# One attention kernel: tables of the group loop redrawn, and the rows of the maxima split on GpSimd and copied on ScalarE

## The reference, cut to what matters

```
scores = einsum('bhqd,bhkd->bhqk', q, k) / sqrt(16)
scores = where(causal, scores, -inf)
attn = softmax(scores, axis=-1)
y = einsum('bhqk,bhkd->bhqd', attn, v)
```

## Time and profile before

| | us |
|---|---|
| median of 3 runs (lowest, highest) | 811.58 (811.36, 812.0) |
| the profiled execution | 810.96 |
| its span | 809.2 |
| granted TensorE clock, mean of the span | 0.998 of full speed |

### The profile page before, as it was taken

One profiled execution on the slowest core, in us unless ns is written; L12 is line 12 of the kernel. 1 busy time (PEld: TensorE's weight loads), 2 busy tenths in 40 slices (PEclk: granted clock), 3 DMA queues, 4 the chain that ended last, 5 costly groups with the idle time before them and its releaser, 6 DMA issues.

```text
span 809.2 us, 15844 instructions
## 1 busy us (share of the span) xinstructions
PE 793.1 (98%) x5286; PEld 534.4 (66%) x5286; DVE 690.7 (85%) x2103; ACT 439.1 (54%) x843; POOL 303.1 (37%) x387
## 2 busy tenths in 40 slices
PE   9999999999999999999999999999999999999996
PEld 6788876876545555555555455555448888888886
DVE  4874767678899999999999999999698888888877
ACT  5333322323479988888988888999861111111110
POOL 0213121221224453535436454555442724334231
PEclk9999999999999999999999999999999999999999
DMA  8316183364613544343454344351321101011111
GB/s 292 118 36 199 41 240 99 98 190 117 149 42 71 107 98 88 85 104 80 90 119 111 77 107 111 74 132 44 105 97 48 46 33 52 26 52 37 42 40 40
DMA packets 44242, 75.53 MB, mean 93 GB/s; under 512 B 13388, under 2 KB 15116, under 8 KB 44172
## 3 DMA queue, kind: packets, MB, share of 16 engines
q1 hardware_dynamic: 44028, 74.51, 35.0%
q10 hardware_dynamic: 144, 0.13, 0.0%
HBM read 48.30 MB, written 21.23 MB: 86 GB/s over the span
## 4 chain that ended last, share of the span: by engine, by line
PE 84%; DVE 6%; ACT 3%; issue 2%; DMA 1%; SPq 1%; POOL 0%; DVEq 0%
PE bank L1879 17%; PE bank L1763 12%; PE bank L1748 11%; PE bank L554 11%; PE bank L556 11%; PE bank L555 11%; ACT pt L1114 2%; PE bank L1692 2%; PE bank L2026 2%; PE bank L1758 2%; PE bank L1708 1%; PE bank L1774 1%; PE bank L1759 1%; DMA ks<-k_parts 1%; PE bank L1947 1%
## 5 line engine op out<-in xcount | busy, mean ns | idle before, releaser
L1114 ACT ACTIVATE pt<-bank 128x512 f32<-128x512 f32 x576 | 305.2, 623 | 52.7 <-PE bank L1748 49.5
L1257 DVE CUSTOM_DVE_ANT_0 bank<-bank,cmask 128x256 f32<-128x256 f32 (+3 forms) x456 | 202.7, 491 | 21.6 <-PE bank L1763 20.2
L1748 PE MATMUL bank<-qs,ks 50*128 50x512 f32 (+3 forms) x768 | 206.1, 376 | 0.9
L1763 PE MATMUL bank<-ks,qs 48*128 48x512 f32 (+3 forms) x712 | 190.3, 392 | 1.9 <-DMA ks<-k_parts 0.9
L1763 PEld LDWEIGHTS bank<-ks,qs 48*128 48x128 f32 x712 | 101.1, 184 | 90.5 <-DVE mx L1260 28.1
L1879 PE MATMUL bank<-pt,vb 128*32 128x512 f32 (+3 forms) x1536 | 157.0, 496 | 0.2 <-ACT pt L1114 0.2
L881 POOL TENSOR_SCALAR_AFFINE_SELECT pt<-pt 128x512 f32<-128x512 f32 (+1 forms) x160 | 85.1, 551 | 158.4 <-ACT pt L1114 158.4
L1748 PEld LDWEIGHTS bank<-qs,ks 50*128 50x128 f32 x768 | 114.9, 185 | 36.1 <-ACT pt L1114 24.9
L1260 DVE TENSOR_REDUCE mx<-bank 128x1 f32<-128x512 f32 x200 | 130.6, 679 | 1.5 <-PE bank L1763 1.1
L800 POOL TENSOR_TENSOR part<-rope,part 128x1024 fp32r<-128x1024 f32 x16 | 38.2, 2388 | 163.8 <-ACT part L972 163.8
L926 POOL TENSOR_TENSOR g<-comb,hr 128x1024 f32<-128x1024 f32 x16 | 30.8, 1925 | 107.4 <-DVE comb L1508 101.9
(11 more groups left out here) (196 smaller groups left out, 1542.6 us busy)
## 6 DMA issues: line engine op xcount, KB each, us to landing
qs<-q_parts SPq DMA_DIRECT2D x34, 256.0 KB, 3.9
ks<-k_parts SPq DMA_DIRECT2D x34, 256.0 KB, 4.3
q_parts<-part SPq DMA_DIRECT2D x32, 256.0 KB, 3.4
k_parts<-part SPq DMA_DIRECT2D x32, 256.0 KB, 3.3
qs<-q_parts SPq DMA_DIRECT2D x34, 128.0 KB, 4.8
ks<-k_parts SPq DMA_DIRECT2D x34, 128.0 KB, 3.4
yv<-yts SPq DMA_DIRECT2D x128, 32.0 KB, 2.3
rspread<-dens SPq DMA_DIRECT2D x64, 64.0 KB, 2.3
```

The source lines that it names most:

```text
L1114: act.activation(pt[k % PT_BUFS][:, h], score_out(g, c), ACT.Exp, scale=float(HD) ** -0.5).then_inc(S("exp_done"), 1)
L1257: last = ve.tensor_tensor_reduce(blk, blk, cmask[:, BANK - nk * P:], 1.0, NEG, ALU.add, ALU.max, mx[m][:, 0, h, qt:qt + 1])
L1748: last = pe.matmul(score_out(g, c)[:, col:col + n_], ks[slot_of(g)][r0:r0 + KX, h // 2, kb * P:(kb + 1) * P], qs[slot_of(g)][r0:r0 + KX, h ...
L1763: last = pe.matmul(out[:, col:col + nk * P], qs[slot][r0:r0 + KR, pr, qt * P:(qt + 1) * P], ks[slot][r0:r0 + KR, pr, k0 * P:(k0 + nk) * P] ...
```

## The change: what it does

1. `BANK_ORDER`, `MAX_AT` and `VALUES_AT` are redrawn. The value steps stood at 8, 12, 17, 22, 25, 27, 32, 35, 38, 41 and stand at 8, 11, 17, 20, 23, 26, 29, 32, 38, 41; the steps (1, [5, 7]) and (1, [1]) change places. The number of tiles, scores and value steps is as it was. `CALC_AT` and `ROWS_AT` are still slots 28 and 30; the last tile of the next group is now issued in chunk 25 (it was 26), the transposition in chunk 30 as before, but now at its start and straight behind the value step of chunk 29.
2. For groups 1 to 15 VectorE only joins the maxima (`join_maxima`). GpSimd makes the high part as a plain rounded copy and the low part by a subtraction, not negated (`split_maxima`, ahead of the work of chunk 26).
3. ScalarE copies the transposed rows from the bank to `mrow` with the factor -1 (`copy_rows`, ahead of the exponential of chunk 30). VectorE's copy is gone. Group 0 is done as before (`first_rows`).
4. The waits follow: TensorE's transposition waits for `rows_low`, SyncE's DMAs and the next user of the bank wait for `rows_copied`, and `reads_before` leaves these uses out.

```diff
-BANK_ORDER = [[[2, 1, 0, 3, EXCESS, 5, JOINED, 4, 6], [2, 0, 6, 1, 5, 4, EXCESS, 3, JOINED]],
-              [[2, 4, EXCESS, 3, 6, 0, 5, JOINED, 1], [3, 4, 6, 0, 5, EXCESS, 2, 1, JOINED]]]
+BANK_ORDER = [[[0, 3, 2, 1, EXCESS, 4, 5, JOINED, 6], [6, 2, 3, 5, 4, 0, EXCESS, 1, JOINED]],
+              [[EXCESS, 5, 6, 0, JOINED, 3, 2, 4, 1], [2, 6, 5, EXCESS, 1, 3, JOINED, 4, 0]]]
...
+JOIN_AT = 26
...
-VALUE_STEPS = [(0, [0]), (0, [2]), (0, [1, 3]), (1, [0]), (1, [6]), (1, [5, 7]), (1, [1]), (1, [4]), (1, [2]), (1, [3])]
+VALUE_STEPS = [(0, [0]), (0, [2]), (0, [1, 3]), (1, [0]), (1, [6]), (1, [1]), (1, [5, 7]), (1, [4]), (1, [2]), (1, [3])]
...
-VALUES_AT = [8, 12, 17, 22, 25, 27, 32, 35, 38, 41]
+VALUES_AT = [8, 11, 17, 20, 23, 26, 29, 32, 38, 41]
...
-MAX_AT = [0, 0, 2, 3, 4, 5, 5, 6, 8, 8, 8, 9, 10, 11, 12, 13, 15, 16, 17, 17, 19, 20, 20, 22, 22, 23, 25, 26, 29, 30, 30, 32, 33, 34, 35, 35]
+MAX_AT = [0, 0, 2, 3, 3, 4, 5, 6, 6, 7, 8, 9, 11, 11, 12, 13, 14, 15, 16, 17, 19, 19, 19, 21, 22, 23, 24, 25, 26, 28, 30, 31, 32, 33, 35, 35]
...
+            def split_maxima(g):
+
+                gp.wait_ge(S("max_joined"), g + 1)
+                rows = mall[:].rearrange("p (a n) -> p a n", a=2)
+                gp.tensor_copy(mneg[:, :, 0], rows).then_inc(S("rows_high"), 1)
+                gp.wait_ge(S("rows_high"), g)
+                gp.tensor_tensor(mneg[:, :, 1], rows, mneg[:, :, 0], ALU.subtract).then_inc(S("rows_low"), 1)
...
+                    if g + 1 < G and c == JOIN_AT:
+                        split_maxima(g + 1)
...
+            def copy_rows(g, use):
+
+                act.wait_ge(S("max_full"), use + 1)
+                act.activation(mrow[g % 3][:], max_out(use)[0:2 * HG * QT, 0:P], ACT.Copy, scale=-1.0
+                               ).then_inc(S("rows_copied"), 1)
...
+                    if g + 1 < G and c == rows_chunk(g):
+                        copy_rows(g + 1, use_of(g, ROWS_AT))
...
-                ve.wait_ge(S("max_joined"), g + 1)
-                rows = mall[:].rearrange("p (a n) -> p a n", a=2)
-                ve.tensor_scalar(mneg[:, :, 0], rows, -1.0, None, ALU.mult).then_inc(S("max_neg_high"), 1)
-                ve.wait_ge(S("max_neg_high"), g + 1)
-                ve.scalar_tensor_tensor(out=mneg[:, :, 1], in0=rows, scalar=-1.0, in1=mneg[:, :, 0],
-                                        op0=ALU.mult, op1=ALU.subtract).then_inc(S("max_negated"), 1)
```

More of the change, by code:

```diff
@@ L249 @@
 EXCESS_USES = [use_of(_g, n) for _g in range(G) for n in slots_with(excess, _g)]
+ROWS_USES = [use_of(_g, ROWS_AT) for _g in range(G - 1)]
 EXCESS_CHUNK = {n: EXCESS_LAG + max(c for c in range(SCORE_BANKS) if FIRST[c] <= n) for n in slots_with(excess, EXCESS_FROM)}
@@ L254, in reads_before, with rows_chunk @@
 def reads_before(use):
-    return use - sum(u < use for u in EXCESS_USES)
+    return use - sum(u < use for u in EXCESS_USES + ROWS_USES)
+def rows_chunk(g):
+    slots = FIRST if g else [first_slots(c) for c in range(SCORE_BANKS)]
+    return max(c for c in range(SCORE_BANKS) if slots[c] <= ROWS_AT)
 def excess_before(g):
@@ L652, in store_max @@
             def store_max(g, use):
-                sp.wait_ge(S("max_read"), reads_before(use) + 1)
+                if g == 0:
+                    sp.wait_ge(S("max_read"), use + 1)
+                else:
+                    sp.wait_ge(S("rows_copied"), g)
                 for par in range(2):
@@ L1262, in max_bank, with join_maxima @@
                 last.then_inc(S("max_read"), 1)
-            def max_rows(g, use):
+            def join_maxima(g, use):
                 if EXCESS_FROM <= g and SLOT_CLEARED[0] + 3 <= g:
@@ L1270, in max_rows, with first_rows @@
                                  ).then_inc(S("max_joined"), 1)
-                ve.wait_ge(S("max_joined"), g + 1)
+            def first_rows(use):
+                join_maxima(0, use)
+                ve.wait_ge(S("max_joined"), 1)
                 rows = mall[:].rearrange("p (a n) -> p a n", a=2)
                 ve.tensor_scalar(mneg[:, :, 0], rows, -1.0, None, ALU.mult).then_inc(S("max_neg_high"), 1)
-                ve.wait_ge(S("max_neg_high"), g + 1)
+                ve.wait_ge(S("max_neg_high"), 1)
                 ve.scalar_tensor_tensor(out=mneg[:, :, 1], in0=rows, scalar=-1.0, in1=mneg[:, :, 0],
                                         op0=ALU.mult, op1=ALU.subtract).then_inc(S("max_negated"), 1)
-            def copy_rows(g, use):
                 ve.wait_ge(S("max_full"), use + 1)
-                ve.tensor_copy(mrow[g % 3][:], max_out(use)[0:2 * HG * QT, 0:P]
-                               ).then_inc(S("max_read"), 1)
+                ve.tensor_copy(mrow[0][:], max_out(use)[0:2 * HG * QT, 0:P]).then_inc(S("max_read"), 1)
             ve.wait_ge(S("c_ld"), 16 * 4)
@@ L1315, in _ @@
                 max_bank(0, w, w)
-            max_rows(0, NMX)
-            copy_rows(0, NMX)
+            first_rows(NMX)
             ve.wait_ge(S("roped"), HEAD["roped"] + 4 * TILES)
@@ L1330, in ve_group @@
                     if slot == CALC_AT and g + 1 < G:
-                        max_rows(g + 1, use_of(g, slot))
+                        join_maxima(g + 1, use_of(g, slot))
                     if slot == FIRST[INVERT_AT] and g > 0:
@@ L1336, in ve_group @@
                         ve.memset(mx[g % 3][:, 0, :, QT - 1], NEG).then_inc(S("slot_cleared"), 1)
-                    if not held(g, slot) or slot in slots_with(excess, g):
+                    if slot == ROWS_AT or not held(g, slot) or slot in slots_with(excess, g):
                         continue
[L1339 to L1343, removed]
+                    n, w = max_tile(slot)
+                    max_bank(g + n, w, use_of(g, slot))
             for w in range(LEAD):
@@ L1725, in free_bank @@
                     pe.wait_ge(S("excess_copied"), EXCESS_USES.index(use - MAX_BUFS) + 1)
+                elif use - MAX_BUFS in ROWS_USES:
+                    pe.wait_ge(S("rows_copied"), ROWS_USES.index(use - MAX_BUFS) + 1)
                 else:
@@ L1779, in trans_rows @@
                     keep_on(out)
-                pe.wait_ge(S("max_negated"), g + 1)
+                if g == 0:
+                    pe.wait_ge(S("max_negated"), 1)
+                else:
+                    pe.wait_ge(S("rows_low"), g)
                 pe.transpose(out[0:2 * HG * QT, 0:P], mneg[:].rearrange("p a s n -> p (a s n)").bitcast(F32),
```

## The result

The kernel after took 799.12 us (median of 4; 798.84 to 800.67) against 811.47 us for the kernel before, measured beside it; the ratio is 0.9851 with a 95% interval of 0.984 to 0.9862. That is 12.3 us faster, where 4.8 were forecast.

The account below looks back on a forecast made before the run. TensorE was taken to lose 2.0 us a group where VectorE and ScalarE are crowded. Gain 14 x 0.4 = 5.6 us less 0.8 for the ends makes -4.8, forecast median 806.8 us; 8-in-10 range 801.5 to 813.2.

Parts of the forecast that it names:

- Where crowding goes: Stretches between value steps: TensorE's loss to crowded VectorE and ScalarE falls from 2.0 to 1.64 us; 0.4 a group taken.
- 1.36 + 0.12 n: Uncrowded time in us of a stretch of n matmuls after a large value step; 0.86 + 0.12 n after a small one.
- three crowdings: After the change, chunks 12 to 17, 24 to 26 and 33 to 2: short by 2.54 us, 1.64 lost after absorption.
- Rows of the maxima leave VectorE: Negation, low part and copy of the rows removed from VectorE, with gaps about 0.75 us of 22.71 per group.
- The copy of the rows: ScalarE's added 64x128 copy, taken as 0.25 us, falls into a wait it has anyway: cost 0; uncovered, 0.25 a group.
- Does the transposition wait?: Whether TensorE's transposition waits for GpSimd's split, 0.6 us after the join: cost 0, with 1.4 us of cover.
- The orders of banks at nothing: Redrawn bank orders change which tile is where, not their sum; costed at 0 (plus or minus 0.5) in the opening phase.
- One switch fewer: Transposition straight behind a value step: costed at nothing; sharing its drain might save 0.18 x 15 = 2.7 us more.
- The ends: Kernel's start and last group: 0.5 us late before group 15, 0.3 in the last group, together +0.8 us.
- Rival A: VectorE was the whole bound, all 0.75 us a group gained: 801.9 us, or 799 with the drain saved; chance 0.18.
- Rival B: Nothing gained, as VectorE's relief at chunk 30 may only lengthen idle time: 811.6 to 812.4, say 811.9 us; chance 0.14.
- Rival C: Slower: each group's first score waits for the rows, 0.45 us a group on a gain of 0.25: 815.2 us; chance 0.18.

Follow-up runs that it names:

- e1: Kernel before with only the four redrawn tables; maxima rows still negated, split and copied on VectorE: 808.85 us, ratio 0.9973.
- e5: Kernel before with the redrawn tables, and GpSimd's mask of chunk 27 waiting for VectorE's low part of the maxima: 803.0 us, ratio 0.9915.
- e15: Kernel after with the split back on VectorE and GpSimd's mask of chunk 27 waiting for it; ScalarE still copies: 806.73 us, ratio 0.9935.
- e2: Kernel after with the four tables of before, so only the moves to GpSimd and ScalarE remain: 811.01 us, ratio 0.9998.
- e3: Kernel after with only the copy of the transposed rows given back to VectorE: 798.72 us, ratio 0.9844.
- e8: Kernel after with only BANK_ORDER of before: 814.98 us, ratio 1.0031, a lower clock having its share in this time.
- e9: Kernel after with VectorE's reciprocal of the denominators, ahead of chunk 15's tiles, done twice: 802.94 us, ratio 0.9899.
- e14: Kernel after with the reciprocal at chunk 11 in place of 15: 799.43 us, ratio 0.9862.
- e6: Kernel after with only the value steps of before, their places and the order of two of them: 817.32 us, ratio 1.0065.
- e7: Kernel after with only MAX_AT of before: 812.62 us, ratio 1.0014.
- e4: Kernel after with only the split of the maxima given back to VectorE; ScalarE still copies: 808.12 us, ratio 0.9966.
- e13: Kernel before with the redrawn tables, the low part replaced by a one-operand multiplication of the joined maxima by 0: 809.24 us, ratio 0.9998.
- e11: Kernel before with VectorE's reciprocal of the denominators done twice: 813.96 us, ratio 1.0034.

## Why the prediction was wrong

**The gain of the period by parts**, all at clock 1.00:

| step | period | what it gives |
|---|---|---|
| before | 23.93 | |
| tables alone (e1) | 23.81 | 0.12 |
| and no collision with the mask (e5) | 23.36 | 0.45 |
| and the copy on ScalarE (e15) | 23.34 | 0.02 |
| and the split on GpSimd (after) | 23.04 | 0.30 |

- **Failed: "Where crowding goes", 0.4 us a group; measured 0.89.** The direction and the places were right in kind, and both terms of the step were too small. The tables were to give 0.36: without the collision they give 0.57 (before to e5). VectorE's relief was to give 0.04 on top: it gives 0.32 (e5 to after). In the prediction's own count, the stretches of 13 matmuls are the only ones well over 1.36 + 0.12 n and 0.86 + 0.12 n, by 0.71 and 0.92 us, 1.63 in all. That this meets the 1.64 forecast is luck: three crowdings were to cost 0.97 (chunks 12 to 17), 0.35 (24 to 26) and 0.32 (33 to 2), and they cost 0.92, 0.12 and 0.71. And the floor they stand on was too high. I had read it from stretches before that looked free and were not: the other eight lie together 0.57 us below it (6 matmuls in 1.95 for 2.08, four in 1.66 for 1.84, eight in 2.18 for 2.32). A fit through rows of a kernel whose engines wait everywhere is no floor. So the period came out at 23.04 where 23.53 was forecast (23.93 less 0.4).
- **"Rows of the maxima leave VectorE", about 0.75 us.** The three instructions are 0.65 us by their own rows, but VectorE's busy time fell by 0.49 a period (after) and 0.53 (e2), not 0.75; no run says where the rest went. The worth was not seen. It is nothing with the old tables (e2) and 0.77 a period with the new ones (e1 to after), 0.45 of it by a collision that I had not considered: the new tables bring VectorE's split onto GpSimd's mask. Putting the split on GpSimd, in order with the mask, removes it.
- **The copy of the rows.** Cost 0 on ScalarE was right (0.27 us, taken for 0.25), and giving it back to VectorE cost nothing (e3, and e5 to e15).
- **Does the transposition wait?** Cost 0 with 1.4 us of cover was wrong by a little: 0.83 us from join to transposition, not 0.6, and about 0.18 us of waiting (1.18 after the value step, where e5 shows 1.00). VectorE's backlog had used up the cover: from the issue of the last maximum (324.76) to the end of the join it takes 2.3 us, not 1.6, and without the wait the transposition would stand 3.0 us after that issue, not 3.6. What these 0.18 us cost is not shown by itself.
- **The orders of banks at nothing.** Wrong: 0.76 us a period (e8), since they decide in which stretch the banks stand that VectorE need not read (by the count of tiles above; no run moves an excess bank by itself).
- **One switch fewer.** The transposition right behind a value step starts 1.00 us after it in e5, as the first score after the value step of 325.08 does in the kernel after (326.08), and takes 0.23 to the next matmul there and 0.20 in the kernel after, 0.23 before. No gain of 0.18 shows. The Trainium skill's sentence on draining ("TensorEngine Tiling (Array Packing)", Key Properties) is not contradicted, but no run isolates a drain, and the price that I put on a shared one does not show.
- **The ends.** +0.8 forecast. Measured between transpositions: up to group 1 it is 1.2 us slower (235.93 for 234.75), of which 0.7 before group 0. The orders of banks are a likely cause but not shown: at full clock that first transposition stands at 206.93 to 207.33 in kernels with the old orders and at 207.26 (e5) to 208.31 with the new. From group 15's on it is 0.8 faster. Sum +0.4.
- **Rival A** (801.9, and 799 with the drain saved, which is the time measured) has the number by luck: VectorE was not the whole bound, as e2 shows, and no saved drain shows. **Rival B** is what the moves do with the old tables. **Rival C** did not come: in the kernel after the first score names the rows' transfer only in front of groups 0 and 15. In e5, where VectorE copies 1.04 us after the transposition, the weights of the first score name it in 11 of 12 groups: in ten by 0.15 to 0.19 us without a longer stretch, in one it holds TensorE for 0.35 us, and that period is 23.60 for 23.35.

**Left open.** Whether VectorE or ScalarE bounds chunks 12 to 17 after the change: both are full in it. e9's dose came too late in it to tell. e14 gives VectorE its reciprocal early in it and leaves it at 3.36 us, which speaks for ScalarE; e8 gives VectorE one tile more and it takes 3.98 us, with ScalarE busy 3.69 of them, which speaks for VectorE. Left open too is why one old table alone (e6, e7) loses nearly the whole gain.

## What to carry to other kernels

When the order of work and the engine of a step change together, the two are not to be priced apart: here each alone gave 0 to 2 us and both 12. A schedule's tables are to be tried as a set: any one of the three put back lost at least 0.76 of the 0.89 us a period. Before moving work in time between VectorE and GpSimd, look at what the other does in SBUF at that moment: a held instruction shows as a longer one, not as a wait. A short instruction on the path can be put on the engine whose long one it would meet, or the long one made to wait for it.

## What the runs showed of the hardware

GpSimd held VectorE up on some instructions that work in SBUF: 0.19 us became 0.67 beside a mask of 0.63 us, for a subtraction with two operands in SBUF (e1; e4 the same) and for a multiplication by a number with one (e13). Each held one ended 0.03 to 0.04 us after the mask. Where VectorE's instruction ran its 0.18 or 0.19 us from the same moment, the mask took 0.68 to 0.69 us, only 0.04 to 0.06 more; where VectorE started 0.06 us or more ahead (e1, e4, e11, e13), the mask kept its 0.64.

Not every instruction of VectorE in SBUF is held. The reciprocal, one operand and the result in SBUF, took 0.34 us inside GpSimd's copy of v in all 14 groups of the kernel before, and also inside a mask:

```profile
588.87 0.80 POOL L881 TENSOR_SCALAR_AFFINE_SELECT pt<-pt 128x512 f32<-128x512 f32 x1 [4.38 <-ACT pt L1114]
...
589.10 0.34 DVE L1326 RECIPROCAL rden<-den 128x32 f32<-128x32 f32 x1
```

(This mask started inside VectorE's subtraction of 128x320, 588.69 to 589.18, and took 0.80 us where most take 0.63.) VectorE's reads of a bank beside GpSimd's work kept their length too: over the groups of the kernel before, a reduction of 128x512 took 0.68 us at the median beside GpSimd and alone.

The Trainium skill says of this in "SBUF — State Buffer", Who interferes with whom: the two share a pair of ports, and the engine that issues first blocks the other for its whole instruction, where VectorE reads two inputs in SBUF or runs in a mode with two ports, which its `tensor_scalar` can enter. The runs agree for VectorE's side; the 0.04 to 0.06 us of the mask is less than the 0.18 us that the rule would add to it. That e13 was held by such a mode fits the reciprocal's being free, but is my reading and was not tested by itself.
